# A two-layer cross-attention and expert network: constants multiplied on TensorE while an expert layer's opening waits

## The chip, the cores and the metric

The kernel runs on one core of one Trainium2 chip. The metric is the device time of one execution in microseconds (us), taken as the median of several runs. All data is in the chip's main memory at the start and the result is written back to it.

## The reference, cut to what matters

`x` is 4 x 512 tokens of 256 features, `ctx` 4 x 1601 rows of 256. Four stages add to `x` one after the other; the tokens are then T = 2048 rows.

```python
x = x + L0_xattn(ctx, layernorm(x), ...)      # 8 heads of 128, keys of ctx and x
x = x + L0_ffn(layernorm(x), ...)             # 8 experts, top 2, capacity 512 tokens per expert
x = x + L1_xattn(ctx, layernorm(x), ...)      # 8 heads of 32
x = x + L1_ffn(layernorm(x), ...)             # 8 experts, top 2, every token served, biases

# an expert layer, in short
scores = xf @ w_router                        # [2048, 8]
top two experts of every token, and their weights
h = gelu(x_of_expert_e @ w1[e])               # 256 -> 1024
y = h @ w2[e]                                 # 1024 -> 256
out[token] += weight * y
```

## The kernel before, in words

The program is four phases in one launch: attention, expert layer 0, attention, expert layer 1. The change is in the function `experts`, which writes both expert layers, and there in TensorE's program only. Each of the five engines has its own instruction stream, written out by hand, with semaphores between them; an engine executes its stream in order, so what stands behind a wait waits too.

**An expert layer's opening.** TensorE transposes the 2048 tokens (L1584), ScalarE and VectorE split the transposes into high and low 16-bit halves, and TensorE computes the router's logits in three products per block (L1604: 96 matmuls of 8 columns). VectorE then selects the two best experts of each token (L1781 to L1803) while ScalarE normalizes the tokens for the row table in memory (L1515). TensorE waits for the selection at `pe.wait_ge(s_sel, 1)` and computes each token's rank within its expert (L1613 to L1616). VectorE turns ranks into slots and into one-hot factors (L1839, L1843), and TensorE multiplies these into the list that says which token sits in which slot (L1645: 32 matmuls in four groups, each of which waits for VectorE's factors). VectorE writes the list as gather indices (L1847).

**The chunks.** The slots are cut into chunks of 256: 16 chunks in layer 0 (two per expert) and 23 in layer 1 (experts start on a chunk border). GpSimd gathers each chunk's rows (L1455) and weights (L1459) by indirect DMA, two chunks ahead; its stream is: gathers of chunks 0 and 1, four base additions that put the old `x` and a bias into the output (L1464), then for each chunk the gathers of the chunk after next and the scatter-add of the results (L1469). For a chunk, TensorE

- turns the rows (`pe_turn`, L1177: four f32 transposes into the bank `psX`), when the gather has landed and the halves of the chunk before are made;
- waits for the halves: ScalarE copies the high half `xh` (L1271), VectorE makes the low half `xl` (L1294);
- computes eight blocks of the hidden layer (`pe_hidden`, L1195 to L1197: six matmuls of 256 columns, into a ring of three banks `psH`), each followed by two GELUs of ScalarE (L1284, L1286) and a difference of VectorE (L1317);
- and multiplies them by the second weights (`pe_output`, L1208, L1209, L1213: six matmuls of 256 columns into `psY`).

The next chunk's turn stands in the middle of a chunk, behind hidden block 3. Chunk 0's turn and its first two hidden blocks stand ahead of the loop and so wait in the open.

**The weights.** Each expert's two matrices come in by DMA from SyncE's queue (L1351) to a staging buffer, a half at a time. ScalarE makes the high 16-bit half of each piece (L1254) and VectorE the low one (L1260); a piece's staging room is loaded again when VectorE has read it. In layer 1 expert 1's second half is split by ScalarE and VectorE right behind the halves of chunk 0's rows, and the pieces of expert n + 2 during chunk n.

**Layer 1 only.** Between the ranks and the index matmuls TensorE also transposes the token weights (L1633) and multiplies them by the output biases (L1624: f32 matmuls with 8 rows), part ahead of the last group of index matmuls and part behind it. ScalarE copies the results out (L1546), and TensorE waits for the last copy before chunk 0's turn.

**The names in the change.** `ones` (all 1.0) and `upper` (a triangle of ones) are constants of 128 x 128 in 16 bits; GpSimd makes them at the layer's start. `psX` is the bank that the turns use; before that it is one of four banks of the first transposes. `psY[3]` holds the router's column sums until VectorE has read them, and from chunk 1 on an output.

TensorE's program around the change:

Of the kernel before, what the change touches and what calls it, by code (L numbers as in the profile page):

```python
# [24 lines left out]
P = 128  # L25
# [946 lines left out]
def experts(nc, X, identf, io, layer, yd, out, pool_sems, small, cleared, load_early=None, early_stats=None):  # L972
# [33 lines left out]
    with ExitStack() as ctx:  # L1006
        tag = f"f{layer}_"

        def sb(name, shape, dt=F32):
            return ctx.enter_context(nc.sbuf_tensor(tag + name, shape, dt))  # L1010
# [54 lines left out]
        ones, upper = sb("ones", [P, P], F16), sb("upper", [P, P], F16)  # L1065
# [25 lines left out]
        psX = ctx.enter_context(nc.psum_tensor(tag + "psX", [P, 512], F32))  # L1091
        psY = [ctx.enter_context(nc.psum_tensor(tag + f"psY{i}", [P, 512], F32)) for i in range(2 * IT)]
# [74 lines left out]

        block = ctx.enter_context(nc.Block(no_gpsimd_drain=True))

        def pe_turn(pe, L, m, p):  # L1170

            n = m * 2 + p
            pe.wait_ge(L.xb[p], m * L.per + L.per)
            pe.wait_ge(L.xL, n + 1)
            for k in range(KC):
                for u in range(IT):
                    ins = pe.transpose(psX[:, k * CH + u * P:k * CH + (u + 1) * P],  # L1177
                                       xb[:, p, u, k * P:(k + 1) * P], identf[:, :])
            ins.then_inc(L.xP, 1)
# [39 lines left out]
        def pe_chunk(pe, L, m, p, experts_of, c, splits, last=False, e=None):  # L1219


            n = m * 2 + p
            if experts_of is None:
                e, e_next = (min((n + i) * E // NC, E - 1) for i in range(2))
            elif L is not main:
                e, e_next = (pe.value_load(experts_of[0:1, bass.ds(c + (0 if last else i), 1)], min_val=0, max_val=E - 1)
                             for i in range(2))
            for f in range(2, FT):
                pe_hidden(pe, L, n, p, e, f)
                if f == 2 and splits and not layer and p == 0:  # L1230
                    pe.wait_ge(s_wl, (m + 2) * PIECES)
                pe_output(pe, L, n, p, e, f - 2)
                if f == 3 and not last:
                    pe_turn(pe, L, m + p, 1 - p)
                if f == 4 and experts_of is not None and L is main:
                    e_next = e if last else expert_of(pe, n + 1)
            if not last:
                pe.wait_ge(L.xL, n + 3)
            if splits and layer:
                pe.wait_ge(s_wl, (n + 3) * PIECES)  # L1240
            elif splits and p == 1:
                pe.wait_ge(s_wl, (m + 2) * PIECES + PH)
            for f in range(2):
                if not last:
                    pe_hidden(pe, L, n + 1, 1 - p, e_next, f)
                pe_output(pe, L, n, p, e, FT - 2 + f)
            return e_next
# [327 lines left out]
        def _(pe):  # L1575
# [22 lines left out]
            for t in range(NT):  # L1598
# [3 lines left out]
                for kk in range(KC):  # L1602
                    for j, (a, w) in enumerate(((xth, wrh), (xth, wrl), (xtl, wrh))):
                        ins = pe.matmul(psY[0][:, t * E:(t + 1) * E], a[:, kk, ts], w[:, kk, :],  # L1604
                                        start=(kk == 0 and j == 0), stop=(kk == KC - 1 and j == 2))
            ins.then_inc(s_lg, 1)


            pe.wait_ge(s_sel, 1)
            NR = NT + layer  # L1610
            flat = sel[:, 0:NR, :].rearrange("p t e -> p (t e)")
# [3 lines left out]
            for t in range(1, NR):  # L1615
                ins = pe.matmul(psR[:, t:NR, :], ones[:, :],  # L1616
                                sel[:, t - 1, :].unsqueeze(1).broadcast_to([P, NR - t, E]), start=False,
                                stop=(t == NR - 1))
            ins.then_inc(s_rk, 1)
            def pe_weighted_bias(i):  # L1620
                if i >= 3:
                    pe.wait_ge(s_wbF, i - 2)
                for u in range(2):
                    ins = pe.matmul(psH[i % 3][:, u * D:(u + 1) * D], wt[:, 2 * i + u, :], b2[:, :], start=True, stop=True)  # L1624
                ins.then_inc(s_wbP, 1)
# [22 lines left out]
            if layer:  # L1648
                for i in range(NB2 + 1, NT // 2):
                    pe_weighted_bias(i)  # L1650
                pe.wait_ge(s_wbF, NT // 2)
            pe_turn(pe, main, 0, 0)
            pe.wait_ge(main.xL, 2)
            pe.wait_ge(s_wl, PIECES + PH)
            for f in range(2):
# [13 lines left out]
            if layer:  # L1669
                pe.wait_ge(s_rest, 1)  # L1670
                pe.wait_ge(main.yF, NC + 2)
                pe.matmul(psY[0][0:1, 0:1], onef[:, :], rest[:, :], start=True, stop=True).then_inc(s_rk, 1)
                pe.wait_ge(s_tab, 2)
                found = pe.value_load(flag[0:1, 0:1], min_val=0, max_val=T * E)
                with pe.If(found > 0):
                    pe.wait_ge(s_done, 1)
                    pe_turn(pe, ties, 0, 0)
                    pe.wait_ge(ties.xL, 2)
                    for f in range(2):
                        pe_hidden(pe, ties, 0, 0, 0, f)  # L1680
                    with pe.Fori(0, NTIE // 2) as m:
                        for p in range(2):
                            pe_chunk(pe, ties, m, p, tie_e, m * 2 + p, False)
# [935 lines left out]
def build(nc, io, out, phases):  # L2619
    with ExitStack() as ctx:  # L2620
# [24 lines left out]
        with ExitStack() as two:  # L2645

            wf = two.enter_context(nc.sbuf_tensor("c_wf", [P, 3, KC, D], F32))
            first = two.enter_context(nc.sbuf_tensor("c_cx0", [P, 4, D], F32))

            def load_early(sp):  # L2650
                for i, name in enumerate(("L1_xattn_Wq", "L1_xattn_Wk", "L1_xattn_Wv")):
                    sp.dma_start(wf[:, i, :, :], io[name].rearrange("(g p) c -> p g c", p=P)).then_inc(s_early, 16)
                sp.dma_start(first[:, :, :], io["ctx_1024"][0, 0:4 * P, :].rearrange("(t p) c -> p t c", p=P)
                             ).then_inc(s_early, 16)

            if "B" in phases:
                experts(nc, X, identf, io, 0, sums[0], out, pool_sems[0], small, cleared, load_early, early_stats)
            if "C" in phases:
                attention1(nc, X, identf, io, sums[0], (wf[:, :, :, :], first[:, :, :], s_early), small,
                           pool_sems[0][1])  # L2660
        if "D" in phases:
            experts(nc, X, identf, io, 1, sums[1], out, pool_sems[1], small, ())
# [24 lines left out]
```

## Time and profile before

| | us |
|---|---|
| median of 3 runs | 2557.98 |
| lowest and highest of them | 2553.86, 2558.17 |
| the profiled execution, its own time | 2552.48 |
| span of the profiled execution, first to last instruction | 2550.7 |
| mean granted clock of TensorE in it (1.00 is full) | 0.969 |

The rows come from one execution taken by the hardware profiler. Times in rows are microseconds from the start of its span, durations without a unit are microseconds, and L with a number is a line of the kernel. PE is TensorE, PEld its weight loads, DVE VectorE, ACT ScalarE, POOL GpSimd, SP SyncE. PEclk is the clock that TensorE was granted, as a share of full speed. In a row of the order of time, the idle time of the engine just before stands in brackets with what ended it; consecutive instructions of the same kind stand in one row with their count.

Expert layer 0 takes about 1437 to 1676 us of the span and expert layer 1 from about 2208 us to the end.

### The profile page before, as it was taken

The numbers are of one execution on the slowest core, as the hardware profiler recorded it, in microseconds if no ns is written. First come the engines' busy times: TensorE is split into PE (matmuls) and PEld (weight loads), VectorE is DVE, ScalarE is ACT, GpSimd is POOL, SyncE is SP. The second block draws the span as 40 slices with busy tenths as digits, with TensorE's granted clock in tenths as the row PEclk, the third lists the DMA queues.
The fourth block names the chain that finished last, engine by engine and source line by source line (L and its number), as shares of the span: only waits on it lengthen the run. The fifth ranks groups of instructions, "written<-read, shape, count | busy, mean of one in ns | idle before, by whom it ended". The sixth has DMA issues, their size and how long they took to land. (4 is left out here: it accounts for less than half of the span.)

```text
span 2550.7 us, 48415 instructions
## 1 busy us (share of the span) xinstructions
PE 2288.7 (90%) x16979; PEld 1394.3 (55%) x16980; DVE 1919.7 (75%) x3499; ACT 1900.7 (75%) x2979; POOL 1809.4 (71%) x1580
## 2 busy tenths in 40 slices
PE   5999999999999999999998589978988888689998
PEld 3454545444544545455544368845555555467777
DVE  7888778887778887777786556558899899676443
ACT  4787887878877878778787546638888889767555
POOL 2687877787777878787778567617787789646554
PEclk9999999999999999999999789989999999779999
DMA  5000000000000000000000365441112010375221
GB/s 151 1 1 1 27 1 1 1 1 1 27 1 1 1 1 1 1 1 1 1 1 1 107 154 144 115 102 45 46 34 50 22 43 11 105 187 140 44 42 24
DMA packets 90655, 104.49 MB, mean 41 GB/s; under 512 B 20626, under 2 KB 79971, under 8 KB 90419
## 3 DMA queue, kind: packets, MB, share of 16 engines
q1 hardware_dynamic: 68180, 78.21, 10.2%
q0 software_dynamic: 21696, 23.16, 5.7%
q8 instruction: 146, 2.39, 0.4%
q14 instruction: 89, 0.73, 0.1%
q10 hardware_dynamic: 544, 0.00, 0.0%
HBM read 66.65 MB, written 23.52 MB: 35 GB/s over the span
## 5 line engine op out<-in xcount | busy, mean ns | idle before, releaser
L432 POOL TENSOR_TENSOR a_acc<-a_acc,a_pf 128x512 f32<-128x512 f32 (+1 forms) x480 | 680.1, 1417 | 280.2 <-ACT a_pf L601 258.5
L906 DVE TENSOR_TENSOR a_pl<-a_pf,a_ph 128x512 f16<-128x512 f32 x448 | 470.3, 1059 | 25.1 <-ACT a_ph L607 25.1
L2221 POOL TENSOR_TENSOR c_pl<-c_pf,c_ph 128x512 f16<-128x512 f32 x320 | 377.2, 1210 | 117.1 <-ACT c_ph L2318 116.7
L601 ACT ACTIVATE a_pf<-a_psS 128x1024 f32<-128x1024 f32 (+1 forms) x288 | 281.1, 976 | 110.0 <-PE a_psS L624 102.5
L882 DVE TENSOR_REDUCE a_mx<-a_psA 128x1 f32<-128x512 f32 x504 | 330.4, 680 | 26.8 <-PE a_psA L681 25.5
L607 ACT ACTIVATE a_ph<-a_psS 128x1024 f16<-128x1024 f32 (+1 forms) x288 | 281.1, 976 | 0.0
L553 ACT ACTIVATE a_psS<-a_mb 128x1024 f32<-128x1024 f32 x255 | 248.6, 975 | 5.0
L1317 DVE TENSOR_TENSOR f_xn<-f_xn 128x256 f16<-128x256 f32 x312 | 130.0, 423 | 152.0 <-ACT f_xn L1286 106.8
L2554 DVE TENSOR_REDUCE c_wf<-c_psA 128x1 f32<-128x512 f32 x384 | 239.4, 677 | 6.2 <-PE c_psA L2390 5.3
L2311 ACT ACTIVATE c_pf<-c_psS 128x1024 f32<-128x1024 f32 x192 | 201.2, 1048 | 49.6 <-PE c_psS L2419 45.1
L776 PE MATMUL a_psO<-a_pl,a_vh 128*128 128x512 f16 (+1 forms) x544 | 206.9, 380 | 8.1 <-POOL a_pl L450 7.9
L770 PE MATMUL a_psO<-a_ph,a_vh 128*128 128x512 f16 (+1 forms) x544 | 206.9, 380 | 8.1 <-DVE a_ol L911 7.3
L622 PE MATMUL a_psS<-a_qh,a_kh 128*128 128x512 f16 (+1 forms) x544 | 206.9, 380 | 0.0
L623 PE MATMUL a_psS<-a_ql,a_kh 128*128 128x512 f16 (+1 forms) x544 | 206.9, 380 | 0.0
L771 PE MATMUL a_psO<-a_ph,a_vl 128*128 128x512 f16 (+1 forms) x544 | 206.8, 380 | 0.0
L624 PE MATMUL a_psS<-a_qh,a_kl 128*128 128x512 f16 (+1 forms) x544 | 206.8, 380 | 0.0
L2318 ACT ACTIVATE c_ph<-c_psS 128x1024 f16<-128x1024 f32 x192 | 201.9, 1052 | 0.0
L681 PE MATMUL a_psA<-a_kh,a_qh 128*128 128x512 f16 x504 | 191.5, 380 | 9.8 <-DVE a_vl L877 9.1
L877 DVE TENSOR_TENSOR a_vl<-a_psA,a_vh 128x256 f16<-128x256 f32 (+1 forms) x266 | 112.0, 421 | 113.1 <-ACT a_vh L518 110.2
L1195 PE MATMUL f_psH<-f_xh,f_w 128*128 128x256 f16 x624 | 172.5, 276 | 3.3 <-DVE f_xl L1294 2.8
L622 PE MATMUL a_psA<-a_wkvh,a_xth 128*128 128x256 f16 (+1 forms) x532 | 146.2, 275 | 31.2 <-DVE a_kl L871 20.7
L1196 PE MATMUL f_psH<-f_xl,f_w 128*128 128x256 f16 x624 | 172.4, 276 | 0.0
(366 smaller groups left out, 6311.4 us busy)
## 6 DMA issues: line engine op xcount, KB each, us to landing
f_stage<-in_L_ffn_w SPq DMA_DIRECT2D x16, 1024.0 KB
f_stage<-in_L_ffn_W SPq DMA_DIRECT2D x16, 1024.0 KB
c_kst<-c_khs SPq DMA_DIRECT2D x64, 100.1 KB, 2.2
a_cx<-in_ctx SPq DMA_DIRECT2D x4, 1536.0 KB
c_cx<-in_ctx SPq DMA_DIRECT2D x12, 512.0 KB, 4.0
f_xrow<-f_xn SPq DMA_DIRECT2D x8, 512.0 KB, 4.6
c_kst<-c_kls SPq DMA_DIRECT2D x32, 100.1 KB, 2.2
X<-in_x SPq DMA_DIRECT2D x4, 512.0 KB, 10.3
```

The costliest lines, as they stand in the source:

```text
L432: g.tensor_tensor(acc[0:k, p, :], acc[0:k, p, :], pf[0:k, q % RF, i, :], ALU.add).then_inc(s_acc, 1)
L553: act.activation(psS[q % 2][0:r, 0:k, :], mb[0:r, :].unsqueeze(1).broadcast_to([r, k, S]), ACT.Copy).then_inc(s_fill, 1)
L601: act.activation(pf[0:r, q % RF, 0:k, :], psS[q % 2][0:r, 0:k, :], ACT.Exp, scale=SCALE).then_inc(s_pF, 1)
L607: act.activation(ph[0:r, q % RP, 0:k, :], psS[q % 2][0:r, 0:k, :], ACT.Exp, scale=SCALE).then_inc(s_pH, 1)
L622: pe.matmul(out, hi, xh_, start=first, stop=False, skip_group_check=onto)
L623: pe.matmul(out, hi, xl_, start=False, stop=False, skip_group_check=onto)
L770: pe.matmul(psO[:, :], vh[0:r, g % 2, j, vs], ph[0:r, q % RP, i, :], start=(j == 0), stop=False)
L776: ins = pe.matmul(psO[:, :], vh[0:r, g % 2, j, vs], pl[0:r, q % RP, i, :], start=False, stop=(j == JT0 - 1))
L882: v.tensor_reduce(mx[:, n % 2, it, c:c + 1], ps[:, 0:KCH[c][1]], AX.X, ALU.max).then_inc(s_fr, 1)
L906: v.tensor_tensor(pl[0:r, q % RP, i, :], pf[0:r, q % RF, i, :], ph[0:r, q % RP, i, :], ALU.subtract).then_inc(s_pL, 1)
L2221: g.tensor_tensor(pl[0:r, q % RP, i, :], pf[0:r, q % RF, i, :], ph[0:r, q % RP, i, :], ALU.subtract).then_inc(s_pG, 1)
L2554: ins = v.tensor_reduce(mx[:, n % 2, it, c:c + 1], ps[:, 0:KCH[c][1]], AX.X, ALU.max)
```

## The change

Three calls of a new helper `pe_spin` are added to TensorE's stream. Each issues matmuls of the constants `ones` and `upper` (128 columns, 16 bits) that start and stop on their own, in turn into the two first quarters of a bank, and signal nothing. Nobody reads what they leave: the next real work on the bank overwrites it.

- 40 into `psX` behind the logits, ahead of the wait for the selection, in both layers.
- ahead of chunk 0's turn, into `psX`: 72 in layer 0 (behind the last index matmul), 40 in layer 1 (behind the last bias product and the wait for its copy).
- 12 into `psY[3]` behind that turn, ahead of the wait for chunk 0's low half.

```diff
+        def pe_spin(pe, bank, times):
+
+            for i in range(times):
+                pe.matmul(bank[:, i % 2 * P:i % 2 * P + P], ones[:, :], upper[:, :], start=True, stop=True)
+
         def pe_turn(pe, L, m, p):
...
             ins.then_inc(s_lg, 1)
+            pe_spin(pe, psX, 40)
             pe.wait_ge(s_sel, 1)
...
                 pe.wait_ge(s_wbF, NT // 2)
+            pe_spin(pe, psX, 40 if layer else 72)
             pe_turn(pe, main, 0, 0)
+            pe_spin(pe, psY[3], 12)
             pe.wait_ge(main.xL, 2)
             pe.wait_ge(s_wl, PIECES + PH)
```

## Rows read from the trace of the kernel before

**Rows 1.** Page: busy time of the engines; granted clock of TensorE in 40 slices.

```profile
PE 2288.7 (90%) x16979; PEld 1394.3 (55%) x16980; DVE 1919.7 (75%) x3499; ACT 1900.7 (75%) x2979; POOL 1809.4 (71%) x1580
...
PEclk9999999999999999999999789989999999779999
```

**Rows 2.** Stretches of layer 0's opening: start:end length, busy us and count, clock, DMA.

```profile
1433.00:1437.00 4.00, 0.04 (x1) 0.00 (x0) 0.00 (x0) 1.36 (x3) 3.08 (x8) 1.00 0.00 0
1437.10:1440.40 3.30, 3.30 (x16) 3.15 (x16) 2.05 (x12) 0.00 (x0) 2.68 (x33) 0.50 0.35 62
1440.50:1443.80 3.30, 0.13 (x1) 0.00 (x0) 0.57 (x1) 1.31 (x4) 0.93 (x1) 1.00 0.89 323
1448.00:1451.00 3.00, 2.97 (x102) 2.82 (x100) 2.38 (x10) 2.74 (x7) 0.00 (x0) 0.50 1.09 384
1482.90:1488.20 5.30, 5.30 (x25) 3.75 (x26) 2.37 (x6) 3.01 (x8) 5.29 (x5) 0.50 0.63 83
1488.30:1500.00 11.70, 11.49 (x106) 10.11 (x105) 6.62 (x15) 7.61 (x21) 5.19 (x6) 1.00 1.18 220
```

**Rows 3.** TensorE in layer 0's opening: start, us, line, operands, count, [idle before <-releaser].

```profile
1457.96 0.28 PE L1613 MATMUL f_psY<-f_first,f_ones 1*128 1x128 f16 x1 [6.99 <-DVE f_sel L1803]
...
1458.25 1.03 PE L1616 MATMUL f_psY<-f_sel,f_ones 128*128 128x120 f16 x15
...
1470.33 1.24 PE L1645 MATMUL f_psY<-f_xn 128*128 128x32 f16 x8 [0.69 <-DVE f_xn L1843]
...
1480.37 1.12 PE L1177 MATMUL f_psX<-identf,f_xb 128*128 128x128 f32 x4 [8.81 <-DMA f_xb<-f_xrow,f_gidx]
...
1482.90 0.39 PE L1195 MATMUL f_psH<-f_xh,f_w 128*128 128x256 f16 x1 [1.42 <-DVE f_xl L1294]
...
1489.45 0.60 PE L1177 MATMUL f_psX<-identf,f_xb 128*128 128x128 f32 x4
...
1500.75 0.60 PE L1177 MATMUL f_psX<-identf,f_xb 128*128 128x128 f32 x4
```

**Rows 4.** Stretches of layer 1's opening, same columns as above.

```profile
2208.60:2211.80 3.20, 3.11 (x15) 3.14 (x16) 2.62 (x8) 0.00 (x0) 1.99 (x30) 0.50 0.16 24
2212.00:2215.20 3.20, 1.44 (x10) 0.84 (x8) 2.65 (x14) 2.81 (x7) 1.93 (x2) 1.00 0.86 288
2259.40:2263.10 3.70, 3.69 (x18) 2.63 (x19) 3.46 (x10) 3.50 (x9) 3.70 (x5) 0.50 0.52 69
2270.00:2272.30 2.30, 0.32 (x4) 0.04 (x2) 0.47 (x1) 1.13 (x3) 0.62 (x1) 1.00 1.14 285
2273.40:2276.70 3.30, 3.30 (x18) 2.29 (x16) 2.81 (x7) 3.30 (x9) 0.00 (x0) 0.50 1.17 246
```

**Rows 5.** TensorE in layer 1's opening, in order of time.

```profile
2228.58 0.29 PE L1614 MATMUL f_psY<-f_sel,f_upper 128*128 128x136 f16 x1 [5.80 <-DVE f_sel L1803]
...
2245.21 2.07 PE L1624 MATMUL f_psH<-f_b,f_wt 8*128 8x256 f32 x4
...
2256.91 1.09 PE L1177 MATMUL f_psX<-identf,f_xb 128*128 128x128 f32 x4 [3.80 <-issue]
...
2259.41 0.39 PE L1195 MATMUL f_psH<-f_xh,f_w 128*128 128x256 f16 x1 [1.42 <-DVE f_xl L1294]
...
2272.30 0.28 PE L1208 MATMUL f_psY<-f_w,f_xn 128*128 x1 [1.98 <-ACT f_xn L1284]
...
2281.97 0.66 PE L1177 MATMUL f_psX<-identf,f_xb 128*128 128x128 f32 x4 [1.25 <-DMA f_xb<-f_xrow,f_gidx]
```

**Rows 6.** ScalarE in layer 1's opening, in order of time.

```profile
2253.15 0.60 ACT L1546 ACTIVATE f_w<-f_psH 128x512 f32<-128x512 f32 x1 [1.11 <-PE f_psH L1624]
...
2271.17 0.63 ACT L1254 ACTIVATE f_w<-f_stage 128x512 f16<-128x512 f32 x1 [3.42 <-DMA f_stage<-in_L_ffn_W]
```

**Rows 7.** Chain of waits that ended last, in layer 1's opening: start, us, what.

```profile
2265.38 1.42 POOL f_xb L1455
...
2267.11 14.82 DMA f_xb<-f_xrow,f_gidx
```

## The prediction, made before the changed kernel had run

> **What bounds the kernel now.** I read the page first. TensorE is busy for 90% of the span, and in most of the 40 slices its digit is 9 [rows 1]: time comes off only where TensorE is on the path, and the clock line shows where its clock is not at full level. Full is 2.4 GHz (1.00 in the rows), half is 1.2 GHz (0.50). The lowest digits of the clock in the second half of the line include the two openings of the expert layers.
>
> Next I cut layer 0's opening into stretches [rows 2] and laid TensorE's own order of time beside them [rows 3]. The reader is to see three waits. The logits end at about 1450.97 us and TensorE stands for 6.99 us until the selection; the index matmuls end at 1471.57 and it stands for 8.81 us until chunk 0's rows are gathered; its four transposes take 1.12 us, and it stands 1.42 us until VectorE has made the low halves. The clock is at half in all of this and stays so from 1482.9 to 1488.2, with TensorE busy all the time: 25 matmuls in 5.30 us, 212 ns each. From 1488.3 on it is at full, 106 matmuls in 11.49 us, 108 ns each. So the first 5.3 us of the layer's dense work run at half speed, and behind them TensorE waits for no gather (the turns at 1489.45 and 1500.75 have no idle time in front), so what it gains there lasts.
>
> Layer 1's opening [rows 4, 5] has the same three waits: 5.80, 3.80 and 1.42 us. But TensorE does not set its length. It stands 1.98 us before 2272.30, because ScalarE stood 3.42 us for a weight load [rows 6], and 1.25 us before the turn at 2281.97. That turn is where the chain of waits passes: it runs through GpSimd's gathers and four base additions to the gather of chunk 2, issued at 2265.38 to 2267.11, which lands 14.82 us later [rows 7].
>
> **The change part by part.** It adds 40 + 72 + 12 matmuls of 128 columns in layer 0, and 40 + 40 + 12 in layer 1. It removes and moves nothing, and no DMA, no semaphore and no other engine's instruction is added.
>
> *The pace of one.* No row has a 16-bit matmul of 128 columns. The nearest are those of 256 columns, 212 ns at half clock and 108 ns at full [rows 2]; halved, 106 and 54 ns. The bounds are 29 ns (102 matmuls in 2.97 us, mostly with 8 columns, at half clock) and 206 ns (16 f32 transposes in 3.30 us) [rows 2]. I take 106 and 54: they are nearest in type and columns.
>
> The Trainium skill, TensorE: Matmul & The Clock Gate, section Back-to-back issue gap, gives about 81 ns for a sustained stream of weight load and matmul of 128 columns; no row here shows one, and by it the spins would fit a little less well at full clock and the sum would be the same.
>
> *First spin, 40.* At half clock 40 x 106 ns = 4.2 us. It fits in 6.99 us of layer 0 and in 5.80 us of layer 1, so it delays nothing: the cover is VectorE's selection chain, and even if it were gone the cost would be 4.2 us at most. The gain could be in the matmuls behind the wait: 1457.96 to 1459.28, 1.3 us at half clock [rows 3], at best 0.65 us less. But 2.8 us of standing follow the spin. I take 0; ends are -0.65 and, at 206 ns each (8.2 us), +1.3. In layer 1 they are covered by ScalarE's and VectorE's weights: 0.
>
> *Second spin, layer 0, 72.* All at half clock it takes 7.6 us from 1471.57 to 1479.2, ahead of 1480.37 where the rows arrive. Clock rises in this trace came after 3.3 us (16 transposes from 1437.1), 3.2 us (2208.6 to 2211.8), 3.7 us (2259.4 to 2263.1) and 5.3 us of dense work [rows 2, 4]. With a rise after 3.2 us it is 30 x 106 + 42 x 54 = 5.5 us, end 1477.0; after 5.3 us, 50 x 106 + 22 x 54 = 6.5 us, end 1478.1. So between 2.3 and 3.3 us of standing are left before the turn. Whether the clock outlives that is open: it stayed at 1.00 through 4.0 us of standing before 1437 and was at 0.50 right after; it was at 1.00 while TensorE stood from 1440.5 to 1443.8 and at 0.50 from 1448 [rows 2]; and 2 us of standing before 2272.3 were followed by 0.50 from 2273.4 [rows 4]. Each time the fall came late, often just as work resumed.
>
> *The turn and the third spin, layer 0.* With the clock up, the four transposes take 0.60 us (as at 1489.45) and not 1.12: -0.5. The 12 matmuls take 1.3 us at half and 0.65 us at full clock, inside the 1.42 us of waiting. Cover gone, they would cost the chunk up to 1.3 us.
>
> *The dense work, layer 0.* Up throughout, 5.3 us at half clock become 2.65: -2.65. If the clock falls at the turn, the spins still start the next rise about 1 us before the dense work does, and some of it is saved. Ends: 0 and -2.65; I take -1.5, a little over the middle. Layer 0 in all: -0.5 - 1.5 = **-2.0 us**, ends 0 and -3.2.
>
> The skill speaks against the first of these terms: TensorE: Matmul & The Clock Gate, Part 4, says that transposes do not bring the full clock. The trace differs: from 2208.6 to 2211.8 TensorE did only f32 transposes, and the clock was 1.00 from 2212 [rows 4]. By the page the -0.5 would be 0 and the sum -1.5.
>
> *Second spin, layer 1, 40.* It starts when ScalarE ends its last copy, 2253.15 + 0.60 = 2253.75 [rows 6]. At half clock it ends at 2258.0, and the rows were there at 2256.91: the turn is 1.1 us late. With a rise after 3.2 us it is 30 x 106 + 10 x 54 = 3.7 us and 0.55 us late, and the turn gives 0.5 back. What is queued behind it: ScalarE's high half and four weight splits, VectorE's low half and its splits, SyncE's load of the next W2 piece that waits for them, and through it ScalarE at 2271.17 and TensorE at 2272.30. All this moves by 0 to 1.1 us. The turn at 2281.97 waited 1.25 us for a gather that was issued long after the first turn, so the delay ends there: 0. By the same row the halved dense work (3.69 us at half clock) gives nothing either. Ends: -1.5 and +1.1.
>
> **Sum:** -2.0 + 0 = -2.0 us. Against the profiled execution's own time, 2552.48 us (span 2550.7 and 1.8 around it), that is 2550.5. The profiled execution stands 5.5 us under the median of the runs shown, 2557.98, so on the median the forecast is 2556.0. About 0.2% (5.1 us) is what a measurement of this kernel can tell from no change.
>
> **The rivals.**
> *A, nothing comes of it.* The clock is down again at the turn, or it does not rise on products of constants, or the 2 us are lost in later falls of the clock that happen to be placed otherwise (the clock line has several [rows 1]). For: the fall that came as work resumed, three times. 2558.0. Chance 0.22.
> *B, everything stays up.* Layer 0 -3.2 and -0.65; layer 1 -0.5 and half of 3.69 = -1.85, if the gather at 2281.97 comes earlier too, and half of the 2.07 us of bias matmuls ahead of its last index group [rows 5], -1.0: -7.2, so 2550.8. Against: 14.82 us of landing fixed by GpSimd's order [rows 7], and the long stand behind each spin. Chance 0.09.
> *C, slower: the second spin outlasts the gather.* Place: layer 1, before chunk 0's turn. Price: +1.1 us at 106 ns each, with the clock at half throughout. It decides from a delay over 1.25 us, the idle time before 2281.97, or if the later weight load also pushes that gather back; then it is +1.1 with nothing gained in layer 0, 2559.1. At the upper bound, 206 ns each, layer 0's 72 take 14.8 us against 8.8 (+6.0), and layer 1's 40 take 8.2 us (+5.1, less 1.25): +9.9, 2567.8. For it: layer 1's spin is longer than its wait by 1.1 us on any pace near 106. Chance 0.14, of it 0.04 for the high end.
>
> **How the numbers follow.** The forecast, layer 0 gains 0.5 to 3.2 us and layer 1 nothing, has 0.55. The runs of before spread by 4.3 us, so its time lies between 2553.86 - 3.2 = 2550.7 and 2558.17 - 0.5 = 2557.7; A adds up to 2558.2 and C's low end up to 2559.3. Range 2550.5 to 2559.5: B's lower half and C's high end are left out, about 0.1, and some of the spread. Faster by over 0.2% is B and a tail of the forecast, 0.11; slower by over 0.2% is C's high end, 0.04; within it 0.85.
>
> **What the profile would show.** Right: in layer 0 the added matmuls end 1 to 3.5 us before chunk 0's turn, 106 ns apart and then 54; the clock in the stretch behind xL is 1.00 for part of what is now 5.3 us; the turn at 1489.45 is some 2 us earlier, and still nothing waits for a gather. In layer 1 the turn comes 0 to 1.1 us late and that at 2281.97 does not move against the index computation. Wrong: added matmuls 200 ns apart; a rank or index stage that becomes shorter; a layer 1 whose turn for chunk 2 moves with the first turn; a total beyond 5 us either way.

## The result, and the profile after

| | before | after |
|---|---|---|
| median, timed side by side (20 runs each), us | 2554.70 | 2561.43 |
| ratio, with its 95% interval | | 1.0023 (1.0017 to 1.0030) |
| the profiled execution, its span, us | 2550.7 | 2562.2 |
| a second set of runs, 23 and 12: medians, us | 2556.86 | 2560.24 |
| ratio there | | 1.0019 (1.0009 to 1.0030) |

By the ratios the change costs about 5 to 6 us. The forecast was 2 us less; the range (up to 2559.5) ends below the median, and the chance given to "slower" was 0.04. The profiled execution of the changed kernel took 2564.02 us, 2.6 us over its median, and that of the kernel before 2552.48, 2.2 us under its own: the two profiles show more of a loss than the medians. Two of the 23 runs of the kernel before in the second set (4416 and 9653 us) and one of `l1_second_again` below (2992 us) ran at a lower granted clock and are left out of the ratios.

Below, "behind the indices" is the time since VectorE began to write the gather indices of that layer. For the profile after, these are the two rows of VectorE's order of time (start, duration, line, operation); before, the same rows stood at 1471.60 and 2247.73.

```profile
1470.39 0.19 DVE L1855 TENSOR_SCALAR f_gidx<-f_psY 128x32 uint32<-128x32 f32 x1 [1.34 <-PE f_psY L1651]
...
2251.79 0.21 DVE L1855 TENSOR_SCALAR f_gidx<-f_psY 128x46 uint32<-128x46 f32 x1 [1.96 <-PE f_psY L1651]
```

**Layer 0.** TensorE's order of time after the change. L1173 is the helper, L1182 a turn (L1177 before), L1200 a hidden block's first product; these rows answer to [rows 3].

```profile
1449.67 3.50 PE L1173 MATMUL f_psX<-f_upper,f_ones 128*128 128x128 f16 x40
...
1470.19 6.89 PE L1173 MATMUL f_psX<-f_upper,f_ones 128*128 128x128 f16 x72
1478.83 0.66 PE L1182 MATMUL f_psX<-identf,f_xb 128*128 128x128 f32 x4 [1.75 <-DMA f_xb<-f_xrow,f_gidx]
1479.33 0.83 PE L1173 MATMUL f_psY<-f_upper,f_ones 128*128 128x128 f16 x12
1480.91 0.28 PE L1200 MATMUL f_psH<-f_xh,f_w 128*128 128x256 f16 x1 [0.75 <-DVE f_xl L1299]
1485.10 0.60 PE L1182 MATMUL f_psX<-identf,f_xb 128*128 128x128 f32 x4
...
1500.68 1.12 PE L1182 MATMUL f_psX<-identf,f_xb 128*128 128x128 f32 x4 [3.63 <-DMA f_xb<-f_xrow,f_gidx]
```

The same in stretches (start:end, length, busy us and count of PE, PEld, DVE, ACT and POOL, granted clock, DMA share, GB/s); they answer to [rows 2].

```profile
1478.80:1479.50 0.70, 0.67 (x8) 0.66 (x8) 0.00 (x0) 0.00 (x0) 0.55 (x1) 1.00 1.16 377
1480.90:1483.80 2.90, 2.89 (x26) 2.43 (x27) 0.92 (x3) 1.28 (x4) 2.59 (x4) 1.00 0.49 128
1499.80:1506.60 6.80, 5.92 (x28) 4.45 (x29) 1.95 (x4) 2.32 (x6) 5.32 (x4) 0.50 0.40 62
```

The first half of this is the best case of the prediction: the clock is up at the turn and in the dense work (26 matmuls in 2.90 us where 25 took 5.30), and chunk 1's turn comes 14.71 us behind the indices, before 17.85: 3.1 us gained. Then chunk 2's turn stands 3.63 us for its gather, and the clock, which falls 0.9 us before that wait ends, is at half for 6.8 us. The turn comes at 30.29 us behind the indices, before at 29.15. Of the gain nothing is left and 1.1 us is lost, and by the layer's last turn (182.85 and 177.36 us behind the indices) 5.5 us in this profile.

**Layer 1.** TensorE's rows, answering to [rows 5], then ScalarE's, answering to [rows 6].

```profile
2257.86 3.88 PE L1173 MATMUL f_psX<-f_upper,f_ones 128*128 128x128 f16 x40 [0.69 <-ACT f_w L1551]
2261.57 0.61 PE L1182 MATMUL f_psX<-identf,f_xb 128*128 128x128 f32 x4
2262.01 0.83 PE L1173 MATMUL f_psY<-f_upper,f_ones 128*128 128x128 f16 x12
2266.37 0.28 PE L1200 MATMUL f_psH<-f_xh,f_w 128*128 128x256 f16 x1 [3.53 <-DVE f_xl L1299]
...
2284.45 0.39 PE L1213 MATMUL f_psY<-f_w,f_xn 128*128 x1 [6.83 <-ACT f_xn L1289]
```

```profile
2264.99 0.60 ACT L1276 ACTIVATE f_xh<-f_psX 128x512 f16<-128x512 f32 x1 [5.68 <-remote]
...
2283.32 0.63 ACT L1259 ACTIVATE f_w<-f_stage 128x512 f16<-128x512 f32 x1 [8.72 <-DMA f_stage<-in_L_ffn_W]
```

`<-remote` means that the profile does not know what ended the wait. The turn is 9.78 us behind the indices (before 9.18): the 0.6 us that the prediction had. But ScalarE makes the high half 3.42 us behind the turn (before: 1.1), then stands 8.72 us for a weight load (before 3.42), TensorE stands 6.83 us behind it (before 1.98), and chunk 2's turn comes 40.81 us behind the indices, before 34.24. The chain of waits no longer runs through GpSimd's gather [rows 7] but through that load:

```profile
2259.32 5.66 another core or an unknown queue
2264.99 0.61 ACT f_xh L1276
2265.62 0.69 DVE f_xl L1299
2266.32 0.22 DVE f_b1e L1307
2266.54 1.20 DVE f_w L1265 x3
2267.73 0.38 issue
2268.11 0.69 DVE f_w L1265
2268.82 14.42 DMA f_stage<-in_L_ffn_W
```

Two theories were drawn from these rows. **P, layer 0:** expert 2's first weight half, which VectorE's split of the chunk before frees, is asked for earlier than before and shares the DMA engines with the gather of chunk 2. **Q, layer 1:** the 0.6 us push a weight load past something, and it lands much later. The rival of both: the added matmuls cost where they stand, or a waiting TensorE with a high clock is throttled elsewhere.

### The profile page after: what moved, and what is told of

Read it like the earlier page. It is cut to its first block and busy times, and to the rows that moved or that the text cites. A ratio compares the mean times of both kernels' runs of the same rounds, so it can differ in the third digit from the quotient of the medians.

```text
span 2562.2 us, 48815 instructions
## 1 busy us (share of the span) xinstructions
PE 2305.7 (90%) x17163; PEld 1413.4 (55%) x17196; DVE 1917.3 (75%) x3499; ACT 1901.5 (74%) x2979; POOL 1806.2 (70%) x1580
## 5 line engine op out<-in xcount | busy, mean ns | idle before, releaser
L906 DVE TENSOR_TENSOR a_pl<-a_pf,a_ph 128x512 f16<-128x512 f32 x448 | 468.6, 1055 | 24.5 <-ACT a_ph L607 24.5
L1200 PE MATMUL f_psH<-f_xh,f_w 128*128 128x256 f16 x624 | 171.0, 274 | 5.9 <-DVE f_xl L1299 4.3
L1202 PE MATMUL f_psH<-f_xh,f_w 128*128 128x256 f16 x624 | 171.0, 274 | 0.0
```

The source lines that it names most:

```text
L906: v.tensor_tensor(pl[0:r, q % RP, i, :], pf[0:r, q % RF, i, :], ph[0:r, q % RP, i, :], ALU.subtract).then_inc(s_pL, 1)
```

## The experiments

Times are medians of runs of the kernel and of the kernel before, timed side by side on one chip; the ratio is this kernel over the kernel before, with its 95% interval. "Turn k" is the turn of chunk k, in us behind the indices, of the profiled execution.

### One layer, one place

`l0_only` has the three spins in layer 0 alone, `l1_only` in layer 1 alone, `sel_only` only the first spin of both layers, `l1_second_only` only the 40 ahead of layer 1's turn.

```diff
+            if not layer:             # l0_only; "if layer:" in l1_only
+                pe_spin(pe, psX, 40)
             pe.wait_ge(s_sel, 1)
...
+            if layer:                 # l1_only; the only call in l1_second_only
+                pe_spin(pe, psX, 40)  # l0_only: "if not layer:", and 72
             pe_turn(pe, main, 0, 0)
...                                    # l0_only, l1_only: the 12 as well
```

> The added matmuls in layer 0 alone, all three places. Theory P (early load): chunk 0 runs at full clock, the weight load of expert 2's first half starts some 5 us sooner and shares the DMA engines with chunk 2's gather; TensorE stands 2 to 4 us before chunk 2's turn and its clock falls behind it: +2 to +5 us against before. Theory Q (overrun): all of the loss is in layer 1, so this gains 1 to 3 us. Rival R (the falls of the clock elsewhere just lie otherwise): within 1 us of before on the median.

> The added matmuls in layer 1 alone. Theory Q: the second group outlasts the gather, chunk 0's turn and with it the second half of expert 1's splits come late, and the weight load behind them queues behind the base additions: +2 to +7 us, with TensorE standing over 4 us for ScalarE's split inside chunk 0. Theory P alone: 0. Together with the kernel of layer 0 alone the two should add up to the whole, +6.7 us.

> Only the first group of 40, in both layers, the other two left out. P and Q both expect no change (within 1 us of before), since its clock is down again by the index matmuls. Rival R expects a shift of 1 to 3 us of either sign.

> Only the group of 40 ahead of chunk 0's turn in layer 1. Q expects the same as layer 1 with all three, +2 to +7 us, since the overrun is here alone. If instead the clock at full level in chunk 0 does the harm, it also shows here; if the third group (12 matmuls) holds the signal of the turn back, this shows nothing.

| kernel | this | before | ratio |
|---|---|---|---|
| l0_only | 2554.67 | 2552.81 | 1.0002 (0.9992 to 1.0012) |
| l1_only | 2556.74 | 2552.81 | 1.0021 (1.0011 to 1.0030) |
| sel_only | 2552.11 | 2552.81 | 1.0001 (0.9991 to 1.0011) |
| l1_second_only | 2556.49 | 2552.81 | 1.0015 (1.0006 to 1.0024) |

The loss is found again with layer 1's second spin alone. The first spins cost and bring nothing that can be measured, as the prediction had it. In layer 0 the gain of the first two chunks is real and gone again. Rows of `l0_only`, the turns of chunks 1 and 2: 14.58 and 30.33 us behind the indices. (This profile is of the slowest of its twelve runs, 2559.59 us.)

```profile
1485.83 0.60 PE L1182 MATMUL f_psX<-identf,f_xb 128*128 128x128 f32 x4
1501.58 1.11 PE L1182 MATMUL f_psX<-identf,f_xb 128*128 128x128 f32 x4 [3.55 <-DMA f_xb<-f_xrow,f_gidx]
```

`l1_second_only` shows layer 1 as the whole change does: the high half 3.24 us behind the turn, and then the wait for the load.

```profile
2258.96 0.60 ACT L1276 ACTIVATE f_xh<-f_psX 128x512 f16<-128x512 f32 x1 [5.48 <-remote]
...
2278.01 0.63 ACT L1259 ACTIVATE f_w<-f_stage 128x512 f16<-128x512 f32 x1 [7.22 <-DMA f_stage<-in_L_ffn_W]
```

### Layer 0's weight load held back, and other spins in layer 1

`l0_hold` is `l0_only`, and SyncE asks for expert 2's first half only when the gather of chunk 2 is in. `l1_short`, `l1_wide` and `l1_narrow` put another spin ahead of layer 1's turn: 24 of 128 columns, 9 of 512 (`upper` read four times over) and 150 of 8.

```diff
-            with sp.Fori(2, E) as e:
+            if not layer:
+                sp.wait_ge(s_xb[0], 64)
+                for half in range(2):
+                    load_weights(2, half)
+            with sp.Fori(2 if layer else 3, E) as e:
```

```diff
+            if layer:
+                pe_spin(pe, psX, 24)       # l1_short
+                pe_wide(pe, psX, 9)        # l1_wide
+                pe_narrow(pe, psX, 150)    # l1_narrow
             pe_turn(pe, main, 0, 0)
```

> The added matmuls in layer 0 alone, and SyncE holds the weight load of expert 2 in layer 0 until chunk 2's rows have landed. Theory P (early load): the gather has the DMA engines to itself again, chunk 2's turn waits 0 to 1.5 us in place of 3.6 and the clock stays up behind it: 1 to 3 us faster than the kernel of layer 0 alone, and 0 to 2.5 us faster than before. If the gather's landing is set by the base additions alone (rival), it lands as late as without the hold and nothing changes against the kernel of layer 0 alone.

> Only the group ahead of layer 1's first turn, cut from 40 to 24 matmuls: some 2.6 us, over 0.5 us before the rows arrive. Theory Q (overrun): turn at the old distance from the indices (9.2 us), ScalarE's copy follows it at once, no change against before. Rival S (it is not the lateness: matmuls in flight ahead of the turn hold its signal back by 1.6 to 2.7 us): the copy is late here too, by over 1 us, and the time is 1 to 4 us over before.

> In place of the 40 matmuls of 128 columns 9 of 512: the same 3.9 us on TensorE with 18 instructions in place of 80. Theory Q and a plain lateness: turn 0.5 to 1.1 us late, and whatever held the signal back with 40 does so here too (about 13.0 us behind the indices in all three profiles). Rival S in the form that the number of instructions matters: the copy follows the turn within 1.2 us and the loss shrinks to under 2 us.

> In place of the 40 matmuls 150 of 8 columns, some 4.0 us at half clock: they do not bring the clock up. Q: same loss as with 40, +2 to +6 us, since only the lateness counts. If the clock at full level in chunk 0 does the harm: no loss. Rival S by number of instructions: the copy is held back at least as long as with 40.

| kernel | this | before | ratio |
|---|---|---|---|
| l0_hold | 2554.76 | 2554.82 | 1.0012 (0.9987 to 1.0037) |
| l1_short | 2554.69 | 2554.82 | 1.0000 (0.9989 to 1.0010) |
| l1_wide | 2557.45 | 2554.82 | 1.0006 (0.9995 to 1.0018) |
| l1_narrow | 2560.19 | 2554.82 | 1.0021 (1.0012 to 1.0030) |

For P: with the load held (`l0_hold`), chunk 2's turn comes at 27.40 us instead of 30.33 in `l0_only`, after 0.45 us of waiting for its gather instead of 3.55:

```profile
1499.63 0.66 PE L1182 MATMUL f_psX<-identf,f_xb 128*128 128x128 f32 x4 [0.45 <-DMA f_xb<-f_xrow,f_gidx]
```

The times of SyncE's request: first the changed kernel, then the kernel before.

```profile
1491.11 0.39 SPq L1356 DMA_DIRECT2D f_stage<-in_L_ffn_w  x1
```

```profile
1496.33 0.39 SPq L1351 DMA_DIRECT2D f_stage<-in_L_ffn_w  x1
```

In the changed kernel it falls between GpSimd's issues for chunk 2:

```profile
1488.08 1.10 POOL L1460 DMA_INDIRECT f_xb<-f_xrow,f_gidx  x1 [0.30 <-issue]
1489.49 1.00 POOL L1460 DMA_INDIRECT f_xb<-f_xrow,f_gidx  x1 [0.30 <-issue]
1490.80 0.94 POOL L1464 DMA_INDIRECT f_xb<-f_wrow,f_gidx  x1 [0.30 <-issue]
1492.05 0.95 POOL L1464 DMA_INDIRECT f_xb<-f_wrow,f_gidx  x1 [0.30 <-issue]
```

In the kernel before it comes 3 us behind the start of the last of the same four. But the time of `l0_hold` is no better than that of `l0_only`, within an interval that one outlier (2587 us) made wide: of the 1 to 3 us that were expected of the hold nothing could be measured.

For Q: 24 constants (turn at 9.30, no later than before by more than 0.12 us) cost nothing and bring nothing; 150 narrow ones, which end far later, cost as much as the change. It is also not the raised clock that costs: in `l1_narrow` it stays at half until 22.4 us behind the indices. `l1_wide` is as late as the change (turn at 9.88) yet the high half comes 1.10 us behind its turn, promptly; the load is late all the same (VectorE has done the next low half of the weights at 30.1 us behind the indices, before at 24.8), and chunk 2's turn at 37.44 is 3.2 us late instead of 6.6. So there are two things in layer 1: a load that lands late, and, with the 40, a signal that comes late. The late load without the late signal (`l1_wide`, 1.0006) costs nothing that is clear of the noise.

`l1_narrow` shows more of the second. Its spin has stops in which the profile finds nothing to wait for:

```profile
2256.35 1.52 PE L1178 MATMUL f_psX<-f_upper,f_ones 128*128 128x8 f16 x51 [0.69 <-ACT f_w L1556]
2258.31 0.29 PE L1178 MATMUL f_psX<-f_upper,f_ones 128*128 128x8 f16 x5 [0.43 <-issue]
...
2261.99 0.26 PE L1178 MATMUL f_psX<-f_upper,f_ones 128*128 128x8 f16 x4 [1.15 <-issue]
...
2263.42 2.19 PE L1178 MATMUL f_psX<-f_upper,f_ones 128*128 128x8 f16 x76 [0.53 <-issue]
```

They end 13.1 us behind its indices; the high half that waited for the 40 starts at 13.0 to 13.2 us.

### Layer 1's base additions later, and a mended kernel

GpSimd's four base additions into `out` are issued from 11.95 us behind the indices on, in every kernel. `late_base_before` and `late_base_after` move them behind the gathers of chunk 2, in the kernel before and in the changed one. `before_hold` is the kernel before with the held load of `l0_hold`; `mended` is `l0_hold` with 24 constants ahead of layer 1's turn.

```diff
-            if layer:
-                g.wait_ge(s_wbF, NT // 2)
-                add_base(lambda q: wb[:, 4 * q:4 * q + 4, :])
-            else:
+            if not layer:
...
+                    if layer:
+                        g.wait_ge(s_wbF, NT // 2)
+                        add_base(lambda q: wb[:, 4 * q:4 * q + 4, :])
```

> No added matmuls; in layer 1 GpSimd issues the base additions behind chunk 2's gathers in place of ahead of them. Theory Q2 (whatever is asked for behind the base additions waits for them, cliff of 5 us and more): chunk 2's rows and the W2 load of expert 2 land 8 us or more sooner, TensorE does not stand before chunk 2's turn; the first scatter then waits for the additions. 0 to 4 us faster. If the landing is set by the volume moved and not by the order: no change.

> The changed kernel with the base additions of layer 1 behind chunk 2's gathers. Q2: the late turn no longer puts the W2 load behind the additions, so layer 1's part of the loss (4 to 5 us) goes away and the kernel is within 3 us of before. If the held-back signal alone costs layer 1 its time, the turn of chunk 2 still comes 3 us late.

> No added matmuls; SyncE alone holds the weight load of expert 2 in layer 0 until chunk 2's rows have landed. Theory P: in the kernel before that load is asked for after the landing anyway, so within 1 us of before. If the hold were what gains by itself: over 1 us faster.

> Layer 0 with all its added matmuls and the hold, layer 1 with 24 in place of 40 ahead of the first turn, nothing else there. P and Q together: both losses are gone, the gain of 1 to 2 us that a full clock gives chunk 0 of layer 0 is left, 0 to 2 us faster than before. Rival R: still 2 us or more slower.

| kernel | this | before | ratio |
|---|---|---|---|
| late_base_before | 2544.09 | 2535.27 | 1.0034 (1.0021 to 1.0048) |
| late_base_after | 2548.31 | 2535.27 | 1.0056 (1.0042 to 1.0070) |
| before_hold | 2534.68 | 2535.27 | 0.9999 (0.9990 to 1.0008) |
| mended | 2535.33 | 2535.27 | 1.0001 (0.9992 to 1.0010) |

Without the additions in its way the load is quick: in `late_base_after` the next low half is done 22.1 us behind the indices, though its load was asked for at 15.1, and chunk 2's turn comes at 29.46 us. With the additions ahead of it and the request at 15.2 (`l1_second_again` below, at the same base) the low half is done at 30.3 and the turn comes at 39.15. So the additions are what makes the load late. That the time lost goes the same way is not shown: `late_base_after` is as much slower than `late_base_before` (1.0056 to 1.0034, five runs each, intervals that overlap) as the change is than the kernel before, though neither has the late load. (It also has layer 0's constants, and waits there 2.09 us for the gather of chunk 2.) Nor is either the better kernel that was expected (`late_base_before` 0 to 4 us faster, `late_base_after` within 3 us): the first scatter must wait for the additions, and chunk 3's gather stands behind it on GpSimd's queue (chunk 3's turn 56.6 us behind the indices, in `before_hold` at the same base 48.1). GpSimd in `late_base_before`:

```profile
2294.36 1.68 POOL L1469 DMA_INDIRECT out<-f_xn,f_sidx  x1 [19.06 <-DMA out<-f_w]
```

`mended` has neither late transfer (turn 2 at 27.28 us in layer 0, 34.66 in layer 1) and takes the time of the kernel before. The constants are then free, and bring nothing that can be measured; up to 2 us had been expected.

### How late is too late, and is it the count

These runs came at a base of 2536 us, 20 us lower than most, like the four before them. `l1_wide12` has 12 of 512 columns, `l1_mid` 20 of 256, and `l1_second_again` is `l1_second_only` once more.

```diff
             if layer:
-                pe_spin(pe, psX, 40)
+                pe_wide(pe, psX, 12)       # l1_wide12
+                pe_mid(pe, psX, 20)        # l1_mid
```

> Layer 1's second spin alone, as 12 matmuls of 512 columns instead of 40 of 128 (as many columns per matmul as four; 1536 more than the 4608 of nine). Expected end of the spin and start of chunk 0's turn: about 10.5 to 11 us behind the gather indices. Theory 'lateness' (the turn's signal is held up when the turn falls too late among the gathers' issues): ScalarE's high half begins 2.5 us or more behind the turn, near 13 us behind the indices, as with 40 of 128. Theory 'count' (it is the number of matmuls issued behind the wait that holds it up): it begins about 1.1 us behind the turn. In either case VectorE's twelfth weight half ends later than in the kernel before (14.1 us behind the indices), and the next piece's weights land over 29 us behind the indices and not at 25.

> Layer 1's second spin alone, as 20 matmuls of 256 columns: the time of 40 of 128, half the instructions. Expected start of chunk 0's turn: about 9.8 us behind the indices, as with 40 of 128. Theory 'lateness': ScalarE's high half begins 2.5 us or more behind the turn. Theory 'count': about 1.1 us behind it. The second chunk's weights land over 29 us behind the indices if the twelfth low half ends 14.5 us or more behind them, else at 25; the time of the kernel follows it: about +1.5 us or nothing.

> The run of layer 1's second spin alone (40 of 128 columns) once more, beside the two above on the same chip. Expected: turn 9.8 us behind the indices, high half 3.2 us behind the turn, twelfth low half 16 to 17 us and the next weights 33 us behind the indices, time 1.001 to 1.002 of the kernel before.

| kernel | this | before | ratio |
|---|---|---|---|
| l1_wide12 | 2536.38 | 2536.04 | 1.0003 (0.9994 to 1.0013) |
| l1_mid | 2536.82 | 2536.04 | 1.0000 (0.9991 to 1.0010) |
| l1_second_again | 2536.44 | 2536.04 | 1.0000 (0.9989 to 1.0011) |

The late load is there in all three. Over all 17 profiles with the base additions in their place it goes by one point of time, in us behind the indices. The load is asked for when VectorE's twelfth low half behind the indices ends (the last of expert 1's second half); the fourth base addition is issued at 14.38 to 14.42 in every one of the 17:

| kernel | load asked for | next low half done |
|---|---|---|
| before, before_hold, mended, mended_again, l0_only, l0_hold | 13.6 to 14.1 | 23.5 to 25.3 |
| sel_only, l1_short | 14.23, 14.25 | 24.5, 24.6 |
| l1_wide12 | 14.40 | 29.9 |
| l1_wide | 14.8 | 30.1 |
| l1_mid, l1_second_again | 15.2 | 30.3 to 30.6 |
| l1_only, l1_second_only, after, after_again | 16.8 to 17.0 | 32.9 to 33.4 |
| l1_narrow | 20.1 | 32.2 |

0.15 us later in the asking is 5 us later in the use. In the profile of the kernel before, the request clears the point by 0.29 us (14.10 against 14.39). The packets show the same. In the 5.4 us behind the request the kernel before (2261.83 to 2267.23) moves 0.59 MB of the load on q1, the queue of SyncE's transfers; the changed kernel (2268.79 to 2274.19) moves nothing on it, and twice as much on q0, GpSimd's. The rows have packets, MB, and the packets' time as a share of 16 engines; the kernel before stands first:

```profile
q0 software_dynamic: 523, 0.52, 70.0%
q1 hardware_dynamic: 578, 0.59, 37.2%
```

```profile
q0 software_dynamic: 1046, 1.04, 123.2%
```

The late signal did not come back: the same 40 of 128 columns, with the turn at 10.31 us, have a prompt high half at this base (1.10 us behind the turn).

```profile
2255.96 1.06 PE L1182 MATMUL f_psX<-identf,f_xb 128*128 128x128 f32 x4
```

```profile
2257.06 0.60 ACT L1276 ACTIVATE f_xh<-f_psX 128x512 f16<-128x512 f32 x1 [3.88 <-PE f_psX L1182]
```

So these runs could not decide between two theories of the late signal: that it goes by the count of products ahead of the turn, or by how late the turn falls among GpSimd's issues. At the base of 2555 `l1_wide` speaks for the count (as late, a quarter as many, no late signal). At this base no kernel has a late signal, so `l1_wide12` and `l1_mid` say nothing of it.

The loss is smaller here as well, too small to measure (1.0000 and 1.0003). At 2536 every later chunk of layer 1 takes 11.3 us. The kernel before, whose layer 1 is that of `before_hold`, waits there 4.09 us for the gather of chunk 2, and its clock is at half for 3.4 us behind that wait, so that from turn 2 (35.1 us) to turn 3 (48.1) it takes 13.0 us. The late kernels have neither and take 11.3. Part of chunk 2's lateness is taken up by that: turn 3 at 48.7 in `l1_wide12` and 50.5 in `l1_second_again`, against 53.4 in `l1_second_only` and 47.0 in the kernel before at 2555.

### The changed and the mended kernel side by side

> The changed kernel as it is, beside the mended one on the same chip. The loss has been measured at a base of about 2555 us for the kernel before; later calls found the kernel before at 2536 us, with every later chunk of layer 1 at 11.3 us. Expected if the base is near 2555: ratio 1.002 again, chunk 2's turn in layer 0 behind a 3 us wait for its gather, chunk 2's turn in layer 1 at 40 us behind the indices. If it is near 2536: the same two late turns (30 us and 39 us behind the indices), but chunk 3 of layer 1 only 2 to 3 us late and no further loss behind it: ratio 1.001 to 1.002. Rival: the loss belonged to the slow base alone, and the ratio at 2536 is 1.000.

> The mended kernel (layer 0's constants with expert 2's weight load held until the gathers of chunk 2 are issued; layer 1 with 24 constants ahead of the turn) beside the changed one. Expected: layer 0's chunk 2 turn 27 us behind the indices without a wait, layer 1's at 34 to 35 us; ratio to the kernel before 1.000, so 0.1 to 0.2% under the changed kernel. Rival: the constants cost elsewhere too, and it is as slow as the changed kernel.

| kernel | this | before | ratio |
|---|---|---|---|
| after_again | 2560.24 | 2556.86 | 1.0019 (1.0009 to 1.0030) |
| mended_again | 2557.14 | 2556.86 | 1.0002 (0.9992 to 1.0013) |

`mended_again` is `mended` once more; its load, too, waits until the rows of chunk 2 have landed, and not until their gathers are issued. The base was near 2555. Turn 2 of layer 1 came at 40.86 us in the changed kernel (high half 3.56 us behind the turn) and at 35.41 in the mended one. In layer 0 the loss is not the same each time: in `after_again` the turn of chunk 2 waited for its gather, but only 1.04 us,

```profile
1498.24 0.66 PE L1182 MATMUL f_psX<-identf,f_xb 128*128 128x128 f32 x4 [1.04 <-DMA f_xb<-f_xrow,f_gidx]
```

and stood at 28.28 us, so part of the gain was kept (0.9 us of the 2.1 that turn 1 had). And `l1_wide12`, whose layer 0 is that of before, turned chunk 2 at 30.62 us, behind a wait of 2.71 us. So the gather of chunk 2 can be late without the constants. The 19 profiles together speak for P. In the five whose turn waits over 1 us for it (3.63, 3.55, 2.09, 1.04, and `l1_wide12`) the load is asked for at 20.6 to 22.5 us behind the indices. In all others but one it is asked for at 23.3 us or later, or held, and the wait is at most 0.45 us. The exception is `l1_mid`, which asks at 22.4 and does not wait; its gathers had been issued 0.55 us earlier. With the constants in layer 0, the four profiles without the hold have the wait; of the three with it two have none and one has 0.45 us. The rival for `after_again`, that the loss belongs to the base, can't be excluded by it, since its base was the one at which the loss had been measured. As far as the runs go, it does: at 2536 the second spin of layer 1 alone costs nothing that can be measured (`l1_second_again`, 1.0000), at 2555 it costs 1.0015, and the whole change was not run at 2536.

## Why the prediction was wrong

**First spins, 0:** right (`sel_only` 1.0001). At a mean clock of 0.66 the 40 took 3.50 us and fit.

**Second spin of layer 0, 5.5 to 7.6 us and 2.3 to 3.3 before the turn:** right in pace (106 ns apart at half clock and 56 at full, taken 106 and 54), and 72 in 6.89 us; the clock rose 5.7 us into the spin, a little later than the 3.2 to 5.3 us it reckoned with, so that 1.75 us were left before the turn. That constants raise the clock, and that it outlives the wait, came out as hoped for.

**Turn -0.5, dense work -1.5:** the first measured -0.46 (1.12 to 0.66 us). The second was too small for this profile and for `l0_only`, where the clock stays up through the dense work, the best case of -2.65. In the other five profiles with these constants the clock is up when the turn begins and falls 0.2 to 2.2 us later, by the start of the dense work, for 3.4 us: the prediction's middle case, the fall that comes as work resumes. Which of the two an execution gets differs for the same kernel (`after` and `after_again`), and nothing here decides it. The clock rule of the Trainium skill, TensorE: Matmul & The Clock Gate, Part 4, by which transposes do not bring the full clock, plays no part in it: the constants did the raising, so that the -0.5 did not hang on that rule as the prediction says.

**"Behind them TensorE waits for no gather, so what it gains there lasts":** this step failed in layer 0. It read the absence of idle time as room. The rows show only that the gather was there in time, not by how much, and the earlier work also asked for a 1 MB weight load 4.0 us earlier behind the indices (1491.11 for 1496.33; 20.7 for 24.7), in the middle of GpSimd's issues for chunk 2. What followed was 3.63 us of waiting and 6.8 us at half clock. `l0_hold` removed the wait by holding the load back alone. The size of layer 0's loss in the median is open: `l0_only` is at 1.0002, so gain and loss about cancel.

**Second spin of layer 1, 0.55 to 1.1 us late:** right (0.6).

**"The delay ends there: 0":** this step failed, and it carries the loss (`l1_only` 1.0021, `l1_second_only` 1.0015, of the change's 1.0023). It held that the delay is absorbed in the 1.25 us before 2281.97; that turn came 6.6 us later behind the indices. Its own list of what is queued behind the spin named the load of the next W2 piece, but moved it "by 0 to 1.1 us", as a load that takes as long whenever it is asked for. Neither holds. The request came 2.9 us later (17.0 for 14.1), 2.3 of them by the late high half, and the load was in use 14.5 us behind its request instead of 9.3. The prediction took the price from the wait of 3.42 us [rows 6] and did not look at what else was on the DMA then: the base additions, which it names beside [rows 7] and whose own row in the kernel before starts between the first turn and the request:

```profile
2259.69 5.38 POOL L1464 DMA_DIRECT2D out<-f_w  x4
```

Rival C named the place and the sign ("if the later weight load also pushes that gather back") and priced it at +1.1 us; the mechanism was a load in use 5 to 9 us later, and chunk 2's turn then had no wait for its gather at all. Its chance should have gone to a mechanism with a cliff, not to a sum of small delays.

That a load asked for behind the fourth base addition is late because it queues behind it is a reading of the table, of the packets and of `late_base_after`; the packets' order was not changed by itself. How the loss divides between the late load and the late signal is not settled. The load alone stands at 1.0006 (0.9995 to 1.0018, `l1_wide`), with the signal at 1.0015 to 1.0021; in profiles the signal is 3 us of turn 2. Why it comes is open.

The forecast also stood on a median of three runs, 2557.98; with 20 runs it is 2554.70. The forecast's -2.0 us against that would be 2552.7, so the miss is 8.7 us and not only the 5.4 between 2556.0 and 2561.43.

## What to carry to other kernels

A wait that is not there in the trace is not slack of known size: before work is moved earlier or later, list the transfers that its end asks for, and look at what is being issued on the other queues within a microsecond of the request. Filling a wait with constants does bring TensorE's clock up, and it was still up at the turn in all seven profiles that had it in layer 0, but throughout the dense work behind only in two of them, and no kernel here became measurably faster by it. A filler that ends at the deadline cost more than it brought; cut it so that it ends well ahead (24 here, not 40). And measure the filler's places apart: of the three calls in two layers only one was found to cost measurable time.

## What was not expected of the hardware

**The clock rises on products of constants and outlives the wait behind them.** In `after`, 72 of 128 columns ran at a mean clock of 0.59; 1.75 us of standing later the turn ran at 1.00. In the seven profiles the clock was at 1.00 after 1.8 to 3.7 us of standing, and in five of them it fell to 0.50 within 2.3 us of the turn's start.

```profile
1470.19:1477.10 6.91, 6.89 (x74) 6.72 (x73) 5.48 (x12) 0.00 (x0) 4.71 (x4) 0.59 0.40 127
```

The products start 106 ns apart at half clock and 56 ns apart at full, each with a weight load of its own. The Trainium skill, TensorE: Matmul & The Clock Gate, section Back-to-back issue gap, gives about 81 ns for such a stream. By that, as an estimate, 72 would take 5.8 us, and they took 6.89; the trace has 81 ns at neither clock.

**ScalarE starts late on what TensorE has made, just behind GpSimd's gather issues, at one base and not at the other.** The ends of TensorE's products are modelled in the profile, so it can't be told whether they or their signals are late, and that the issues cause it is not shown: they are there at both bases. It is not the change's alone. ScalarE in the kernel before, in the middle of layer 1, stands 3.59 us for a hidden block whose last product TensorE began at 2373.15 (0.27 us long), until 0.83 us behind the last of four gather issues; TensorE then waits 1.15 us for the GELU. ScalarE, GpSimd and TensorE:

```profile
2376.58 0.47 ACT L1284 ACTIVATE f_xn<-f_psH,f_b1e 128x256 f16<-128x256 f32 x1 [3.59 <-PE f_psH L1197]
```

```profile
2374.81 0.94 POOL L1459 DMA_INDIRECT f_xb<-f_wrow,f_gidx  x1 [0.30 <-issue]
```

```profile
2377.19 0.28 PE L1208 MATMUL f_psY<-f_w,f_xn 128*128 x1 [1.15 <-ACT f_xn L1284]
```

In layer 1 more than 2.5 us pass between the starts of two GELUs 19 to 21 times in the profiles of `before`, `after_again` and `mended_again`, and 2 or 3 times in those at the base of 2536 (`before_hold`, `mended`, `l1_second_again`), where the longest wait of this kind in layer 1's later part is 0.9 us. The change's late high half has the same signature: it comes 1.03 to 1.26 us behind the last of the opening's eight gather issues, in the four runs that had it. What makes the base 2536 in some sets of runs and 2555 in others, on the same chip, was not found.
